# Moving set-up work between GpSimd and ScalarE, and dropping early waits, in a graph layer with an on-chip edge sort

## The reference

```python
def _L0_gnn_ref(h, row, col, dist, eW1, eb1, eW2, eb2, nW1, nb1, nW2, nb2):
    edge_in = jnp.concatenate([h[row], h[col], dist], axis=1)      # 64 + 64 + 1
    e = jax.nn.silu(edge_in @ eW1 + eb1)                           # 128
    e = jax.nn.silu(e @ eW2 + eb2)
    agg = jax.ops.segment_sum(e, row, num_segments=h.shape[0])
    node_in = jnp.concatenate([h, agg], axis=1)
    out = jax.nn.silu(node_in @ nW1 + nb1) @ nW2 + nb2
    return out
x = _layernorm(x + _L0_gnn_ref(x, src, dst, edge_weight1, ...), axis=-1)
```

## Time and profile before

| | us |
|---|---|
| Median of three runs | 633.36 (631.66 to 633.81) |
| The profiled execution | 633.18 |
| Its span, first to last instruction | 631.4 |
| Busy: PE, POOL, DVE, ACT | 565.6, 432.4, 427.7, 363.6 |

### The profile page before, as it was taken

The page is one execution under the profiler, slowest core; times in us unless marked ns, Lnnn a source line. Parts: engine busy times, 40 slices in busy tenths (PEclk is TensorE's granted clock), DMA queues, the critical chain, the costliest instruction groups (busy, mean ns, idle before and its releaser), DMA issues.

```text
span 631.4 us, 15748 instructions
## 1 busy us (share of the span) xinstructions
PE 565.6 (90%) x4943; PEld 483.1 (77%) x4943; DVE 427.7 (68%) x1298; ACT 363.6 (58%) x829; POOL 432.4 (68%) x465
## 2 busy tenths in 40 slices
PE   3896889899999999999999999999998888879795
PEld 3665587788887899898788987897777777769674
DVE  6866899898689768778777678677643433223346
ACT  3475266355655675766565566556556666657554
POOL 4325777567777777777777777777777777777740
PEclk9995789889989999999999899989999999999997
DMA  5301111112212212221212122211221222221211
GB/s 120 102 14 43 51 51 51 43 44 55 51 51 52 55 51 54 54 56 52 55 52 56 51 56 52 56 51 52 56 56 51 56 55 52 56 54 53 55 39 52
DMA packets 17219, 34.23 MB, mean 54 GB/s; under 512 B 8133, under 2 KB 9352, under 8 KB 17017
## 3 DMA queue, kind: packets, MB, share of 16 engines
q0 software_dynamic: 14080, 28.86, 17.2%
q1 hardware_dynamic: 2594, 3.40, 2.1%
q10 hardware_dynamic: 468, 0.96, 0.6%
HBM read 30.73 MB, written 2.40 MB: 52 GB/s over the span
## 4 chain that ended last, share of the span: by engine, by line
POOL 37%; PE 29%; issue 16%; DVE 14%; ACT 2%; DMA 1%; DVEq 1%; POOLq 0%; ACTq 0%
POOL q_rows L819 37%; PE layer_ps L832 13%; PE sort_ps L832 9%; PE seg_ps L832 5%; DVE load_hot L1362 3%; DVE col_hot L1356 1%; PE turn_ps L978 1%; DVE row_hot L1357 1%; DVE agg L1433 1%; DMA q_rows<-q_table,q_index 1%; DVE count L1213 1%; ACT p_table L592 1%; DVE hot L1418 1%; DVE count L1254 0%; DVEq L1425 0%
## 5 line engine op out<-in xcount | busy, mean ns | idle before, releaser
L819 POOL DMA_INDIRECT q_rows<-q_table,q_index x440 | 419.5, 953 | 158.4 <-issue 129.8
L659 ACT ACTIVATE e<-layer_ps 128x512 f32<-128x512 f32 x110 | 65.7, 597 | 200.6 <-PE seg_ps L832 196.0
L1433 DVE TENSOR_TENSOR agg<-agg,seg_ps 128x125 f32 x416 | 93.2, 281 | 115.2 <-PE seg_ps L832 113.8
L832 PE MATMUL layer_ps<-hotT,p_table 128*128 128x128 bf16 x1320 | 161.5, 228 | 0.2
L832 PE MATMUL layer_ps<-ident_f,q_rows 128*128 128x128 f32 x440 | 129.2, 294 | 26.6 <-DMA q_rows<-q_table,q_index 25.8
L832 PEld LDWEIGHTS layer_ps<-hotT,p_table 128*128 x1320 | 124.9, 100 | 22.6 <-issue 1.4
L832 PE MATMUL seg_ps<-hot,e 128*128 128x125 f32 x880 | 122.1, 282 | 4.4 <-DVE agg L1433 4.4
L832 PE MATMUL layer_ps<-w_sb,h 128*128 128x128 f32 x880 | 125.3, 287 | 0.0
L832 PEld LDWEIGHTS layer_ps<-w_sb,h 128*128 128x128 f32 x880 | 113.3, 198 | 4.6
L832 PEld LDWEIGHTS seg_ps<-hot,e 128*128 128x128 f32 x880 | 106.9, 192 | 6.1 <-issue 3.8
L832 PEld LDWEIGHTS layer_ps<-ident_f,q_rows 128*128 128x128 f32 x440 | 64.9, 148 | 37.6 <-DMA q_rows<-q_table,q_index 36.7
(11 more groups left out here) (209 smaller groups left out, 470.6 us busy)
## 6 DMA issues: line engine op xcount, KB each, us to landing
q_rows<-q_table,q_index POOLq DMA_INDIRECT x440
q_table<-q_in_sb SPq DMA_DIRECT2D x1, 896.0 KB
x_sb<-in_x_dram ACTq DMA_DIRECT2D x1, 700.0 KB
q_table<-q_in_sb SPq DMA_DIRECT2D x1, 504.0 KB
out_dram<-x_sb SPq DMA_DIRECT2D x2, 224.0 KB
out_dram<-x_sb SPq DMA_DIRECT2D x1, 252.0 KB
w_in<-in_edge_weight_dram SPq DMA_DIRECT2D x1, 185.9 KB
dst_i<-in_dst_dram SPq DMA_DIRECT2D x1, 185.9 KB
```

The lines of the kernel that those rows point to most:

```text
L659: A.activation(e2[:, m % 2, :], e_of(m)[:], ACT.Silu).then_inc(e2_ready, 1)
L819: P.indirect_dma_start(q_rows[:, g % RING, j, :], None, q_table, bass.IndirectOffsetOnAxis(ap=q_index[:, GT * g + j:GT * g + j + 1], axis= ...
L832: return nc.tensor.matmul(o, lhsT, rhs, start=start, stop=stop, **kw)
L1433: D.tensor_tensor(o, o, seg_ps[:, j * LO:(j + 1) * LO], ALU.add).then_inc(agg_added, 1)
```

## The change

Five edits. The selector `column_sel` is made by ScalarE, not by GpSimd, behind a first small copy. ScalarE also clears `agg[1]`, after the first spread copy of chunk 2 and ahead of the main loop. x is loaded on SyncE's queue, directly behind src of chunk 0, not on ScalarE's. The waits ahead of groups 1, 2 and 3 of the gathers are gone. SUM and `pick` work in three parts (a fifth, to three fifths, the rest) and not in two halves, and the turn of the windows (`TURN_SLOT`) goes from slot 7 to slot 8.

```diff
-TURN_SLOT, SPREAD_SLOT = 7, 10
+TURN_SLOT, SPREAD_SLOT = 8, 10
...
+        def place_bounds(k):
+            n = segments(k)
+            return [0, n // 5, n * 3 // 5, n]
...
             load_nodes(*CODED[0], src_in)
+            for a, b in ROWS:
+                sp.dma_start(x_sb[a:b, :], x.rearrange("(p b) f -> p (b f)", b=WIN)[a:b, :]).then_inc(x_in, 16)
...
         def _(act):
             A = nc.scalar
-            act.wait_ge(ident_ready, 1)
-            for a, b in ROWS:
-                act.dma_start(x_sb[a:b, :], x.rearrange("(p b) f -> p (b f)", b=WIN)[a:b, :]).then_inc(x_in, 16)
+            act.wait_ge(fills_ready, 1)
+
+            A.activation(wc_part[0:1, 0, 0:1], ones[0:1, 0:1], ACT.Copy)
+            act.wait_ge(ident_ready, 2)
+            A.activation(column_sel[:], ident_b[0:NMAX, 0:NMAX].unsqueeze(2).to_broadcast([NMAX, NMAX, WIN]), ACT.Copy) \
+                .then_inc(column_sel_ready, 1)
...
-            act.wait_ge(fills_ready, 1)
             clear(agg[0])
...
             load_coded(1)
             copy_spread(2, 0)
+            clear(agg[1])
             for m in range(GROUPS):
...
             P.memset(fills[0][0], 1.0).then_inc(fills_ready, 1)
-            pool.wait_ge(ident_ready, 2)
-            P.tensor_copy(column_sel[:], ident_b[0:NMAX, 0:NMAX].unsqueeze(2).to_broadcast([NMAX, NMAX, WIN])) \
-                .then_inc(column_sel_ready, 1)
...
-            P.memset(agg[1][:], 0.0).then_inc(agg_clear, 1)
...
-                if g == 1:
-                    pool.wait_ge(window_ready, 1)
-                if g == 2:
-                    pool.wait_ge(offsets_ready, 2)
-                if g == 3:
-                    pool.wait_ge(step_ready, 1)
-                    pool.wait_ge(window_ready, 2)
...
-                    if t in (0, n // 2):
-                        pe.wait_ge(place_ready, 2 * k + 1 + (t > 0))
+                    if t in place_bounds(k):
+                        pe.wait_ge(place_ready, 3 * k + 1 + place_bounds(k).index(t))
...
-                    half = segments(k) // 2 * EP
-                    for a, b in ((0, half), (half, wide)):
+                    bounds = place_bounds(k)
+                    for a, b in ((t0 * EP, t1 * EP) for t0, t1 in zip(bounds, bounds[1:])):
```

## The result

The changed kernel takes 627.10 us (median of six runs, 625.39 to 628.45) against 633.62 us for the kernel before, measured beside it: a ratio of 0.9896, 95% interval 0.9872 to 0.9919. That is 6.6 us less (5.1 to 8.1). The forecast was 628.6 us, in a range of 625.3 to 631.6 us. The profiled execution took 626.75 us with a span of 624.9 us, so its 6.4 us under the execution profiled before stand for the median.

What follows compares the result with a forecast made beforehand. Bounds: a serial head to about 74 us, TensorE and VectorE by turns to 212.71 us, then GpSimd's gathers. Terms 4.0 (head) + 0.6 (three parts) + 0 + 0 = 4.6 us, 633.2 to 628.6 us, range 625.3 to 631.6.

Steps and rivals of the forecast that it cites:

- the stall: GpSimd's 4.80 us wait before group 3 moves to a TensorE wait of 4 to 5 us at group 5.
- the last hold: TensorE's last hold of GpSimd above 0.6 us, before 212.71 us, was to come 4 to 5 us earlier.
- The cast and the fills: Kernel start: without GpSimd's selector and clear, fills and first cast end sooner; VectorE gains 3.3 to 5.1 us.
- The head's 4.0 us: Serial head: smaller gain of VectorE's chain and x's load with TensorE's steps, 4.0 us, bounds 2.4 to 5.1.
- The second clear on ScalarE: After the spread copy ending at 53.21 us: 2.81 us hidden in ScalarE's 3.88 us idle time.
- The removed waits and the turn's slot: GpSimd's first groups and the windows' turn: 0 us each; bounds for the turn -1.0 to 0.9.
- The three parts' 0.6 us: Sums in chunks 0, 1 and 3 gain together 0.6 us, bounds 0 to 1.2; later chunks nothing.
- the third stage: Behind 212.71 us, GpSimd's fixed pace of gathers; work saved there by any other engine is worth nothing.
- The wait for weights or x (630.1 us): Rival in the head: weights or x land late and become the wait; 630.1 us, chance 0.2.
- ScalarE's clear as the culprit (633.4): Rival: ScalarE's clear, not GpSimd's, held the first cast; no change, 633.4 us, chance 0.03.
- The slower case (635.3): Rival in chunk 1: gathers delay some 18 short VectorE steps by 0.37 us each; 635.3 us, chance 0.05.
- TensorE's clock: Rival before 212.71 us: two fewer low-clock stretches, 625.3 us, chance 0.08; two more, 632.0 us, chance 0.07.

Runs made afterwards that it cites:

- Number 6: Kernel before with only the second aggregate's clear moved from GpSimd to ScalarE, behind chunk 2's first spread copy: 630.22 us, ratio 0.9951.
- number 1: Kernel before with only the head's edits (selector and second clear on ScalarE, x on SyncE's queue): 628.14 us, ratio 0.9913.
- number 2: Kernel before with only the three waits of GpSimd's first groups removed: 633.14 us, ratio 0.9991.
- number 4: Changed kernel with the three waits of GpSimd's first groups put back: 625.76 us, ratio 0.9882 to the kernel before.
- number 8: Changed kernel with the turn of the other chunks' windows back in slot 7: 626.83 us, ratio 0.9892 to the kernel before.
- Number 7: Changed kernel with the sums and the selection in two halves again: 629.11 us, ratio 0.9931 to the kernel before.
- number 12: Kernel before with three parts of the sums and selection in chunks 2 to 8 only: 631.96 us, ratio 0.9980.
- number 5: Kernel before with ScalarE's clear of the first aggregate moved behind chunk 2's first spread copy, GpSimd's clear kept: one execution, 633.58 us beside 633.55.
- number 9: Kernel before with nine more tiny VectorE instructions ahead of its first wait for the fills: 632.54 us, ratio 0.9997.
- number 10: Kernel before with three parts of the sums and selection in chunks 0 and 1 only: 632.67 us, ratio 0.9992.
- number 3: Kernel before with only the sums and the selection in three parts: 631.13 us, ratio 0.9963.
- number 11: Changed kernel with x on ScalarE's queue, ahead of the small copy and the selector: 628.20 us, ratio 0.9925 to the kernel before.

## Why the prediction held, and where its sum was off

The forecast lay 1.5 us above the measured time. The head's mechanism was right. Two terms were too low, one of them because a step of the argument was wrong, and a longer stretch at TensorE's lower clock took 1.6 us of the difference back; so the number came out as close as it did partly by luck. Of the signs that were named, the cast, the first product, the first gather, the stall and the last hold came as forecast or nearly so; the last gather (5.6 us earlier, not 4 to 5) and the tail (0.9 us shorter, not unchanged) did not.

**The cast and the fills: right.** The cast was to end between 4.1 and 5.9 us and ended at 4.58. Number 6 prices the removed clear alone at 3.1 us, and number 1 the head as a whole at 5.5.

**The head's 4.0 us: mechanism right, value low.** The prediction took the smaller gain of two chains, with x at 8.0 us. TensorE could start on x at 7.61 us, so its two steps were done ahead of VectorE's total at 11.91 us. The gain was then VectorE's own, 4.6 to 4.9 us, still inside the term's bounds (2.4 to 5.1). Two sizes were off: x's landing, 6.4 us from issue in the sum, where TensorE began on x after 5.97 us, and TensorE's two steps, 4.67 us in the sum and 4.17 us in the trace (7.61 to 11.78 us). The weights were wanted at 10.14 us and used at 10.36, against "about 10".

**The second clear on ScalarE: right.** It is hidden, as the timeline of after shows:

```profile
48.86 2.81 ACT L539 ACTIVATE agg<-ones 128x3125 f32<-128x3125 f32 x1
...
53.12 0.22 ACT L642 ACTIVATE hot<-w_parts 128x12 bf16<-128x12 bf16 x1 [1.45 <-DVE hot L1415]
```

ScalarE still idles 1.45 us behind it (3.88 before).

**The removed waits and the turn's slot: right, 0 each** (numbers 2, 4 and 8).

**The three parts' 0.6 us: wrong, 2.3 us.** The direct part was about right: in chunk 0, SUM to SLOTS took 3.30 us before and 3.13 after, 0.17 us against 0.2. The step that failed is "Later chunks stand beside other TensorE work: nothing", and with it the sentence that in the third stage work saved by any engine but GpSimd is worth nothing. VectorE's SUM makes GpSimd's gathers longer. In the timelines of before, VectorE's two instructions of 625 columns and the gathers beside them, for two of the four chunks behind 212.71 us:

```profile
351.60 1.65 DVE L1254 SCALAR_TENSOR_TENSOR count<-count,base_col,in_win 125x625 f32<-125x625 f32 x2
352.53 1.54 POOL L819 DMA_INDIRECT q_rows<-q_table,q_index  x1 [0.30 <-issue]
...
412.22 1.65 DVE L1254 SCALAR_TENSOR_TENSOR count<-count,base_col,in_win 125x625 f32<-125x625 f32 x2
413.17 1.52 POOL L819 DMA_INDIRECT q_rows<-q_table,q_index  x1 [0.30 <-issue]
```

The same in after:

```profile
346.17 1.78 DVE L1251 SCALAR_TENSOR_TENSOR count<-count,base_col,in_win 125x250 f32<-125x250 f32 x3
346.41 1.06 POOL L816 DMA_INDIRECT q_rows<-q_table,q_index  x1 [0.30 <-issue]
347.77 1.00 POOL L816 DMA_INDIRECT q_rows<-q_table,q_index  x1 [0.30 <-issue]
...
406.70 1.78 DVE L1251 SCALAR_TENSOR_TENSOR count<-count,base_col,in_win 125x250 f32<-125x250 f32 x3
407.93 1.37 POOL L816 DMA_INDIRECT q_rows<-q_table,q_index  x1 [0.30 <-issue]
```

A gather takes 0.94 us. In before each of the four chunks stretches one, to 1.44, 1.30, 1.54 and 1.52 us: 2.04 us over. In after the stretched ones are 1.15, 1.04, 1.06, 1.00 and 1.37 us: 0.92 us over. Number 7, with halves, has 1.23, 1.56, 1.37 and 1.43 us, 1.83 over; number 12, with three parts, 1.04, 1.37, 1.00 and 1.00 us, 0.65 over. So by these four traces shorter SUM instructions give GpSimd 0.9 to 1.4 us, in the very stretch where nothing but GpSimd counts. The other traces agree: the gathers beside SUM are 1.2 to 1.7 us over in numbers 1, 2, 5, 6, 9 and 10, which have halves in these chunks, and 0.5 to 0.8 us in numbers 3, 4, 8 and 11, which have three parts. The Trainium skill, "SBUF — State Buffer", section "Who interferes with whom", says that a VectorE instruction with two inputs in SBUF contends with a GpSimd instruction that reads SBUF; SUM has two such inputs (`count`, `in_win`), the gather reads its indices there (`q_index`), and the rows agree.

The rest of the 2.3 us lies in the tail, where the place is shown and the cause is not. From the start of the last gather to the span's end, before and numbers 1, 2, 5, 6, 7 (halves) and 10 (three parts in two chunks only) take 22.1 to 22.5 us, and after and numbers 3, 4, 8, 11 and 12 (three parts) 21.4 to 21.7. The weight loads of TensorE for the last group, the first one on the gathered rows and the one that follows the first layer, of before:

```profile
612.34 0.14 PEld L832 LDWEIGHTS layer_ps<-ident_f,q_rows 128*128 128x128 f32 x1 [0.46 <-DMA q_rows<-q_table,q_index]
...
613.93 0.97 PEld L832 LDWEIGHTS seg_ps<-hot,e 128*128 128x128 f32 x8
```

then of after:

```profile
606.20 0.20 PEld L829 LDWEIGHTS layer_ps<-ident_f,q_rows 128*128 128x128 f32 x1
...
607.44 0.97 PEld L829 LDWEIGHTS seg_ps<-hot,e 128*128 128x128 f32 x8
```

Before, TensorE waits for the rows until 3.47 us after the last gather's start. After, it comes to them 2.90 us behind that start with no wait: 0.57 of the 0.9 us. The other 0.35 us lie in the first layer itself, which takes 1.59 us before (612.34 to 613.93) and 1.24 us after (606.20 to 607.44). The queues that moved data in before from 610 to 611 us (packets, MB, share of 16 engines) show what else was under way:

```profile
q0 software_dynamic: 30, 0.06, 19.1%
q14 instruction: 1, 0.01, 4.1%
```

A fetch of instructions goes through the same DMA engines while the last gather's rows do. In after that fetch comes from 600 to 601 us, ahead of the last gather (603.30):

```profile
q14 instruction: 1, 0.01, 2.3%
```

In number 9 it comes at 606 to 607 us, ahead of 609.57. So nine VectorE instructions alone move it, and number 9's profiled tail is short too (21.4 us). The two go together in all fourteen traces. Where the fetch on q14 starts 1.6 to 1.8 us behind the start of the last gather (before, 1, 2, 5, 6, 7, 10), TensorE begins on the rows 3.1 to 3.5 us behind that start and its first layer takes 1.6 us; where the fetch starts 1.5 to 3.9 us ahead (after, 3, 4, 8, 9, 11, 12), it is 2.8 to 2.9 us and 1.2 to 1.3 us. Yet number 9's time shows no gain that can be told; its bounds (up to 1.1 us) leave room for the 0.9. In its one profile TensorE is at the lower clock from 176.6 to 183.4 us, and the way from group 5 to the last hold is 1.2 us longer than before's, which takes back what the tail gives; whether the timed runs have that is not known. That the tail shortens in the profile is shown; that the packet is what delays the rows, and that the timed runs have the whole of it, stays open.

**The rivals.** The wait for weights or x (630.1 us) did not come: 0.2 us. ScalarE's clear as the culprit (633.4) fell with numbers 5 and 6. The slower case (635.3), short steps each delayed by gathers, did not come either: chunk 1's steps stayed near 0.2 us, with one of 0.40 us. TensorE's clock did take something. By the table, the span's 6.5 us are 4.9 up to the first gather (with the 0.2 of chunk 0's parts), 1.0 up to group 5, 1.6 lost up to the last hold, 1.25 and 0.9. The 1.0 us goes with a higher granted clock between the first gather and group 5 (0.71 in mean, 0.60 before) and with chunk 1's parts, and is not taken apart. The 1.6 us are the longer low stretch between 171 and 178 us, and traces of kernels without the head's edits show its price. Number 5, which differs from before only in when ScalarE clears the first aggregate, shows the same doubling:

```profile
177.60:181.00 3.40, 3.40 (x20) 3.29 (x20) 2.12 (x12) 0.00 (x0) 2.58 (x3) 0.50 0.19 57
181.00:184.40 3.40, 3.40 (x25) 3.21 (x24) 1.00 (x5) 0.00 (x0) 1.39 (x3) 0.50 0.07 21
```

From group 5 to the gather of the last hold, before and numbers 2, 7 and 12, where the stretch lasts 3.4 us, take 139.3 to 139.6 us; after and numbers 5, 8 and 10, where it lasts 6.8 us and the other low stretches on the way are the same, take 141.2 to 141.3: 1.6 to 2.0 us for one more such stretch, near the 1.7 us at which the prediction had priced one. Numbers 1, 4, 6 and 9, which have it but one low stretch less near 120 to 130 us, take 140.4 to 140.9, number 3, with two doubled stretches, 142.1, and number 11, with none at all, 138.2. As the doubling comes in number 5 and stays away in number 7, it is not a lasting price of the head's edits; how often the timed runs have it is not known.

## What to carry to other kernels

Ask of an engine that sets the pace not only whom it waits for but whose instructions stretch its own: the mean of a gather hid four that took a third to two thirds longer beside one VectorE operation. Cutting a long two-input VectorE instruction into parts can pay there, even where its result is not awaited. In a serial head, price every chain that has to come earlier (here VectorE's and x's load), since the gain is the smallest of them.

## What the runs showed of the hardware that was not expected

A gather's issue on GpSimd went from 0.94 to as much as 1.56 us (number 7) beside VectorE's `SCALAR_TENSOR_TENSOR` of 625 columns, and to at most 1.37 us beside three of 250 and 500 columns. Nine tiny VectorE instructions at the start of the kernel (number 9) shifted a fetch of instructions some 600 us further on, from beside the last gather to ahead of it. One more stretch of 3.4 us at TensorE's lower clock came and went between kernels that do not differ in that place (before and number 5), and cost about 1.7 us.
